# Attention with a routed expert layer: choice and placement of experts moved behind the next maxima on VectorE

## The chip, the cores and the metric

The kernel runs on one core of one Trainium2 chip. The metric is the device time of one execution in microseconds, lower is better. Five engines work side by side and meet only at semaphores: TensorE (PE in the rows, its weight loads PEld), VectorE (DVE), ScalarE (ACT), GpSimd (POOL) and SyncE (SP), which issues most transfers. Each engine does its own instructions strictly in the order in which they are written.

## The reference, cut to what matters

```python
x = x + xattn(layernorm(x), ctx, Wq, Wkv_expand, Wout)     # 32 batches of 112 rows, 512 wide, 16 heads, causal
x = x + ffn(layernorm(x), ...)

# in ffn, xf = all 3584 rows:
probs = softmax(xf @ gate_w.T, axis=1)                      # 8 experts
top_p, top_i = top_k(probs, 2)                              # two experts for each row
h = silu(xf @ fc1_e.T) * (xf @ fc2_e.T)                     # expert e, 352 wide
y = sum over the two experts of top_p * (h @ proj_e.T)
shared = (silu(xf @ s1.T) * (xf @ s2.T)) @ sp.T             # shared expert, 1408 wide
y = y + sigmoid(xf @ shared_gate.T) * shared
```

## The kernel before, in words

The program has three stages. The first does attention, the second layer norm, the router and the lists of rows for each expert. The second runs 63 tiles of 128 rows through their experts. The third does the shared expert and adds all up. Products are made from three fp32r products of high and low halves. The change touches the first stage alone, which lies between 0 and about 440 us.

The first stage is a software pipeline written out by hand. Its loop is `body(g)` on every engine: group g has four steps j = 0 to 3, and step (g, j) starts batch t = 4g + j; there are 8 groups with batches, and two more groups in which the rest drains while the shared expert's first block is computed. In one step TensorE does, in this order: the causal mask (line 925) and the scores (L935) of batch t, then for batch t - 1 the transposes of the exponentials (L944), of the inverse sums `rinv_wide` (L952) and the product with the values (L963), for batch t - 3 the transposes of the normed rows `xn` (L972), for batch t - 2 the output product (12 matmuls of L815), for batch t - 3 the router (L1001), then queries, keys and values of later batches (21 matmuls of L815). Once a group, at j = 2, `ranks` adds four small matmuls behind the router (L902, L903), which count the rows chosen before each row.

VectorE's `step(g, j)` does: the reciprocal of the last batch's sums (L1664); the maxima of the scores (`smax`, L1671, and `minus_max`, L1673), on which ScalarE's exponentials wait; `stats1` for the next batch (L1556, L1559); `rows_copy`, the copy of the normed rows out of PSUM (`xn2T`, L1629), on which the router waits; the low half of a later x; `attnT` (L1694); `x1` (L1703); `logits` and, at j = 2, the ranks' copy (L1642); `stats2`; the low half of `attnT` (L1715). At the end stands `choices(g, j)`: at j = 0 `choose(g - 1, 0)`, at j = 1 `choose(g - 1, 1)`, at j = 3 `place(g - 1)`. These are 10, 12 and 6 very small instructions on [112, 32] numbers, each of which waits for the one before. In group 7 they already stand behind the maxima of the following step.

GpSimd does in a step: `rinv_wide` (L1456), then `inverse_root` and `xn` of batch t - 3 (L1407, L1409, L1464), at j = 0 and 2 the halves of the context (L1418, L1420), `scaled_root` of batch t + 1 (L1407, L1409), and at j = 0 to 2, from group 3 on, three, three and two indirect transfers that write row numbers into the experts' lists (`scatter`, L1427); at j = 0 of groups 4 to 7 the row numbers are moved on first (L1436).

PSUM banks 4 to 7 are taken in turns. The table `TURNS` has for each result its bank and its place among the users of that bank, and `take` and `wait_emptied` count by it. The ranks' result lies in bank 4 before, behind the output product that `x1` reads. SyncE stores the routes of group g - 1 at the end of `body(g)`.

Of the kernel before, what the change touches and what calls it, by code (L numbers as in the profile page):

```python
# [62 lines left out]
class Turns:  # L63
# [5 lines left out]
    def there(self, g, j, lag):  # L69

        if j < 0 or lag is None:
            return g == 0
        return 0 <= g * TB + j - lag < self.batches
# [15 lines left out]
def build_program(nc, x, xT, ctxT, wq, wkv, wout, gates, w_experts, w_shared, out):  # L89
# [19 lines left out]
    with ctx:  # L109
# [382 lines left out]

        def is_last(n):

            return isinstance(n, int) and n == NG
# [56 lines left out]
        def _(sp):  # L552
# [41 lines left out]

            def body(g):
                for j in range(TB):
# [20 lines left out]
                    if there(g, j, 3):  # L617
# [12 lines left out]
                if routes(g):  # L630
                    sp.wait_ge(S["slots_ready"], g - 1)
                    sp.dma_start(route_rows[bass.ds(g - 2, 1)].rearrange("a s b f -> (a s) b f"),
                                 route_of(g - 1)[:, :, :]).then_inc(S["route_stored"], 16)
# [175 lines left out]
        def _(pe):  # L809
# [87 lines left out]
            def ranks(g, j):  # L897
# [3 lines left out]
                b = take(g, j, "rank")  # L901
# [193 lines left out]
            wait_emptied(pe, NG + 1, 2, "rank")  # L1095
# [275 lines left out]
        def _(pool):  # L1371
# [76 lines left out]
            def body(g):  # L1448
                for j in range(TB):
# [7 lines left out]
                    if there(g, j, 3):  # L1457
                        inverse_root(mv2, rs2, (j + 1) % 2, "stats2", "rstd2_made", t - 2)
                        if there(g, j, 5):
                            wait_filled(pool, g, j - 2, "normT")  # L1460
                            pool.wait_ge(xn2_stored[(j + 1) % 2], 16 * (2 * g + (j - 3) // 2))
                        pool.wait_ge(S["rstd2_made"], 2 * (t - 2))
                        settled(pool)
                        pool.tensor_scalar(xn2[:, (j + 1) % 2, :], x1[:, (j + 1) % 2, :], mv2[:, (j + 1) % 2, 0:1], rs2[:, (j + 1) % 2, 1:2],  # L1464
                                           ALU.subtract, ALU.mult).then_inc(S["xn2_ready"], 1)
# [6 lines left out]
                    if routes(g - 1) and before(g, NG + 1):  # L1472
                        if j == 0:
                            if isinstance(g, int) and g == 3:
                                pool.wait_ge(S["lists_zeroed"], 16)
                            else:
                                move_ids(g - 3)
                        if j < 3:
                            scatter(g - 2, ITEMS[3 * j:3 * j + 3])
                if isinstance(g, int) and g >= NG:  # L1480
# [70 lines left out]
        def _(dve):  # L1551
# [79 lines left out]
            def logits_out(g, j):  # L1631
# [5 lines left out]
                if j == 2 and routes(g):  # L1637

                    b = turns.bank("rank")
                    wait_filled(dve, g, j, "rank")  # L1640
# [16 lines left out]
            def step(g, j):  # L1657
# [16 lines left out]
                if is_late(g) and (g == NG - 1 or (g == NG and j == 0)):  # L1674
                    choices(*((g, j - 1) if j else (g - 1, TB - 1)))
# [41 lines left out]
                if is_late(g, 0) or not is_late(g, 2) or (j < TB - 1 and not is_late(g)):  # L1717
# [67 lines left out]
            def place(n):  # L1785

                link, count = chain("slot_step", (n - 1) * SLOT_STEPS)
                wait_emptied(dve, n + 1, 2, "rank")
# [308 lines left out]
```

## Time and profile before

| | us |
|---|---|
| median of 3 runs | 1524.58 (1521.63 to 1526.14) |
| the profiled execution | 1526.51 |
| its span, first to last instruction | 1524.7 |
| TensorE busy in the span | 1483.0 (97%) |
| VectorE, ScalarE, GpSimd busy | 854.7, 653.7, 585.3 |

The profiled execution is 0.1% above the median, inside the range of the runs. The granted TensorE clock over the span is 0.997 of full speed. Times in the rows are microseconds from the span's start, and engine names are those given above. "Step (4, 1)" below is the stretch from the first `smax` instruction of that step to the first of the next one.

### The profile page before, as it was taken

To read this page: it belongs to the slowest core of one execution; us is meant where nothing else is said; L and a number is where in the kernel's file an instruction comes from. 1 tells how busy PE (TensorE), PEld (TensorE's weight loads), DVE (VectorE), ACT (ScalarE), POOL (GpSimd) and SP (SyncE) were. 2 spreads that over 40 slices of the span, in tenths; PEclk is the share of its full clock that TensorE was granted. 3 is DMA by queue.
4 is the path that set the end of the run, shared out by engine and by line. 5 is a ranking of instruction groups with operands and counts; after the bars stand their busy time and mean duration, and the time that the engine had idled before them with its cause. 6 is when DMAs were issued, how large, how long until landed. Compare 5 with 4: busy or idle time off the path is not lost.

```text
span 1524.7 us, 28281 instructions
## 1 busy us (share of the span) xinstructions
PE 1483.0 (97%) x10026; PEld 1257.6 (82%) x10026; DVE 854.7 (56%) x1460; ACT 653.7 (43%) x1836; POOL 585.3 (38%) x503
## 2 busy tenths in 40 slices
PE   7999999999989999999999999999999999999999
PEld 5787777777778899999999999887888888888887
DVE  5566667667665578877867867545223322233322
ACT  6998888888864323333332332432111111111111
POOL 3333446545553277865865965112100001000010
PEclk9999999999999999999999999999999999999999
DMA  7244455545346489867778765553213012030110
GB/s 242 67 117 116 98 112 102 112 106 119 81 113 138 105 325 340 282 239 272 283 244 278 251 219 186 193 198 98 86 28 111 28 48 77 14 110 28 62 49 28
DMA packets 102905, 217.44 MB, mean 143 GB/s; under 512 B 43696, under 2 KB 48816, under 8 KB 98064
## 3 DMA queue, kind: packets, MB, share of 16 engines
q1 hardware_dynamic: 91184, 184.71, 38.8%
q0 software_dynamic: 11616, 31.35, 7.1%
q8 instruction: 63, 1.03, 0.3%
q14 instruction: 42, 0.34, 0.1%
HBM read 168.86 MB, written 47.17 MB: 142 GB/s over the span
## 4 chain that ended last, share of the span: by engine, by line
PE 81%; ACT 6%; issue 6%; DVE 4%; POOL 2%; DMA 1%; SPq 0%; DVEq 0%; POOLq 0%; ACTq 0%
PE psum L815 60%; PE psum L1134 11%; ACT probs L1239 4%; PE psum L894 2%; PE psum L1036 2%; PE psum L935 1%; PE psum L1060 1%; ACT probsT L1228 1%; PE psum L944 1%; POOL xn L1464 1%; DVE smax L1671 1%; PE psum L972 1%; PE psum L1001 1%; PE psum L963 0%; PE psum L925 0%
## 5 line engine op out<-in xcount | busy, mean ns | idle before, releaser
L1544 POOL DMA_INDIRECT routed<-expert_out_dram,slot_b x56 | 56.4, 1007 | 480.2 <-DVE slot_b L1993 327.9
L1239 ACT ACTIVATE probs<-psum,minus_max,rs 112x112 f32<-112x112 f32 x512 | 222.7, 511 | 2.4 <-DVE minus_max L1673 2.4
L2011 DVE TENSOR_TENSOR h_s<-psum,silu_s 128x512 f32<-128x512 f32 x66 | 45.7, 692 | 302.9 <-PE psum L815 298.6
L815 PE MATMUL psum<-nT_hi,ws_hi 128*128 128x512 f32 x528 | 209.4, 397 | 3.2 <-DVE nT_lo L1934 2.9
L815 PE MATMUL psum<-nT_lo,ws_hi 128*128 128x512 f32 x528 | 209.4, 397 | 0.0
L815 PE MATMUL psum<-nT_hi,ws_lo 128*128 128x512 f32 x528 | 209.2, 396 | 0.0
L1516 POOL DMA_INDIRECT xg<-normed_dram,tile_ids x63 | 149.9, 2380 | 35.7 <-DMA tile_ids<-lists_dram 12.7
L815 PE MATMUL psum<-wj_hi,gT_hi 128*128 128x352 f32 x504 | 162.8, 323 | 0.0
L815 PE MATMUL psum<-wj_hi,gT_lo 128*128 128x352 f32 x504 | 162.3, 322 | 0.0
L815 PE MATMUL psum<-wj_lo,gT_hi 128*128 128x352 f32 x504 | 161.8, 321 | 0.0
L1359 ACT ACTIVATE silu_s<-psum 128x512 f32<-128x512 f32 x66 | 39.4, 598 | 244.1 <-PE psum L815 244.1
L1239 ACT ACTIVATION_READ_ACCUMULATOR probs<-psum,minus_max,rs 112x1 f32 x512 | 139.7, 273 | 0.0
L1362 ACT ACTIVATE hs_hi<-h_s 128x512 fp32r<-128x512 f32 x66 | 41.7, 632 | 200.4 <-DVE h_s L2011 200.4
L1919 DVE TENSOR_TENSOR wj_lo<-wj_raw,wj_hi 128x2816 fp32r<-128x2816 f32 x35 | 121.6, 3476 | 8.9 <-POOL wj_hi L1499 7.2
L815 PEld LDWEIGHTS psum<-nT_hi,ws_hi 128*128 128x128 f32 x528 | 99.6, 189 | 27.6 <-DVE nT_lo L1934 3.4
L815 PEld LDWEIGHTS psum<-nT_hi,ws_lo 128*128 128x128 f32 x528 | 99.6, 189 | 24.0
L1499 POOL TENSOR_SCALAR wj_hi<-wj_raw 128x2816 fp32r<-128x2816 f32 x34 | 87.3, 2569 | 83.4 <-issue 76.1
L815 PEld LDWEIGHTS psum<-nT_lo,ws_hi 128*128 128x128 f32 x528 | 99.5, 188 | 23.5
L1134 PE MATMUL psum<-ws_lo,hs_hi 128*128 128x512 f32 x264 | 103.4, 392 | 0.0
L1134 PE MATMUL psum<-ws_hi,hs_hi 128*128 128x512 f32 x264 | 103.3, 391 | 0.0
L1134 PE MATMUL psum<-ws_hi,hs_lo 128*128 128x512 f32 x264 | 102.9, 390 | 0.0
L815 PEld LDWEIGHTS psum<-wj_lo,gT_hi 128*128 128x128 f32 x504 | 94.9, 188 | 2.6
(253 smaller groups left out, 3426.2 us busy)
## 6 DMA issues: line engine op xcount, KB each, us to landing
wj_raw<-in_w_experts SPq DMA_DIRECT2D x35, 1408.0 KB
wj_raw<-in_w_experts SPq DMA_DIRECT2D x35, 768.0 KB, 5.7
wj_raw<-in_w_shared SPq DMA_DIRECT2D x22, 768.0 KB, 5.5
expert_out_dram<-y_c SPq DMA_DIRECT2D x63, 256.0 KB
base<-x_dram SPq DMA_DIRECT2D x8, 1024.0 KB, 5.8
xT_raw<-in_xT SPq DMA_DIRECT2D x32, 224.0 KB, 5.5
x_in<-in_x SPq DMA_DIRECT2D x32, 224.0 KB, 5.4
x_res<-in_x SPq DMA_DIRECT2D x32, 224.0 KB
```

Source lines behind the costliest of these rows:

```text
L815: mm = pe.matmul(out_ap, u, v, start=(n == 0), stop=(n == last))
L894: mm = pe.matmul(bank(j), u, v, start=(c == 0 and q == 0), stop=(c == SC - 1 and q == 2))
L1036: mm = pe.transpose(psum[:, XT_BANK, c * P:(c + 1) * P], xg[b][:, c * P:(c + 1) * P], ident[:, :])
L1134: mm = pe.matmul(bank(j), u, v, start=(i == 0 and q == 0), stop=(i == SC - 1 and q == 2))
L1239: done = act.activation(probs[:, j % 2, 4 * r + m, :], psum[0:SEQ, r, m * SEQ:(m + 1) * SEQ], ACT.Exp, bias=minus_max[:, r, m:m + 1], scal ...
L1359: act.activation(silu_s[:, :], bank(b), ACT.Silu).then_inc(emptied_b[b], 1)
L1362: act.activation(hs_hi[:, i % 2, :], h_s[:, :], ACT.Copy).then_inc(S["hs_hi_made"], 1)
L1499: pool.tensor_scalar(wj_hi[b][:, FC_COLS], wj_raws[b][:, FC_COLS], 1.0, 0.0, ALU.mult, ALU.add).then_inc(S["wc_hi_made"], 1)
L1516: pool.indirect_dma_start(out=xg[b][:, :], out_offset=None, in_=normed_dram, in_offset=bass.IndirectOffsetOnAxis(ap=tile_ids[:, k % ROUND: ...
L1544: pool.indirect_dma_start(out=routed[:, b % 2, c, :], out_offset=None, in_=expert_out_dram, in_offset=bass.IndirectOffsetOnAxis(ap=slot_b[ ...
L1919: dve.tensor_tensor(wj_lo[b][:, FC_COLS], wj_raws[b][:, FC_COLS], wj_hi[b][:, FC_COLS].bitcast(F32), ALU.subtract).then_inc(S["wc_split"], 1)
L2011: dve.tensor_tensor(h_s[:, :], bank(b), silu_s[:, :], ALU.mult).then_inc(emptied_b[b], 1)
```

## The change

On VectorE, `choices` of a step now always stands behind the maxima of the following step, and no longer at the end of its own; group 7 and the first step of group 8 had this order already, so it is new for groups 2 to 6. On GpSimd, `inverse_root` and `xn` move from the second place of a step to its last: batch t - 2 at the end of step t, in place of batch t - 3 near the start of it. That puts them behind `scatter`. The ranks' result moves from bank 4 to bank 7, where it stands behind the product with the values, which `attnT` reads, and ahead of the keys. SyncE stores the routes of a group at j = 0 of a later group, behind the place where they are now made. TensorE's order stays as it was.

```diff
+              *([((_j, "rank", 0), "rank", 7)] if _j == 2 else []),
...
-        TURNS += [((_j, "rank", 0), 2 * TB, 4)]
+        TURNS += [((_j, "rank_tail", 0), "tail", 4)]
...
+            def store_routes(n):
+                sp.wait_ge(S["slots_ready"], n)
+                sp.dma_start(route_rows[n - 1], route_of(n)[:, :, :]).then_inc(S["route_stored"], 16)
...
+                    if j == 0 and 3 <= g <= NG:
+                        store_routes(g - 2)
...
-                if routes(g):
-                    sp.wait_ge(S["slots_ready"], g - 1)
...
+                if g >= NG:
+                    store_routes(g - 1)
...
-                    if there(g, j, 3):
-                        inverse_root(mv2, rs2, (j + 1) % 2, "stats2", "rstd2_made", t - 2)
-                        if there(g, j, 5):
-                            wait_filled(pool, g, j - 2, "normT")
...
+                    if there(g, j, 2):
+                        inverse_root(mv2, rs2, j % 2, "stats2", "rstd2_made", t - 1)
+                        if there(g, j, 4):
+                            wait_filled(pool, g, j - 1, "normT")
+                            pool.wait_ge(xn2_stored[j % 2], 16 * ((t - 2) // 2))
+                        pool.wait_ge(S["rstd2_made"], 2 * (t - 1))
...
-                if is_late(g) and (g == NG - 1 or (g == NG and j == 0)):
+                if t and (g < NG or (g == NG and j == 0)):
                     choices(*((g, j - 1) if j else (g - 1, TB - 1)))
...
-                if is_late(g, 0) or not is_late(g, 2) or (j < TB - 1 and not is_late(g)):
+                if is_late(g, 0):
                     choices(g, j)
```

VectorE before, at the end of step (2, 3) and the start of (3, 0); `rt_eq`, `route` and `slots_i` are the six instructions of `place`.

```order
L1715 TENSOR_TENSOR aT_lo<-attnT,aT_hi 128x448
L1792 TENSOR_TENSOR rt_eq<-rt_rank,rt_one 112x32
L1793 TENSOR_REDUCE route<-rt_eq 112x4
L1794 CAST slots_i<-route 112x4
L1792 TENSOR_TENSOR rt_eq<-rt_rank,rt_one 112x32
L1793 TENSOR_REDUCE route<-rt_eq 112x4
L1794 CAST slots_i<-route 112x4
L1664 RECIPROCAL rinv<-rsum 112x16
L1671 TENSOR_REDUCE smax<-psum 112x8
```

The same place of VectorE after (line numbers are 12 higher there).

```order
L1676 RECIPROCAL rinv<-rsum 112x16
L1683 TENSOR_REDUCE smax<-psum 112x8
L1685 TENSOR_SCALAR minus_max<-smax,rs 112x8
L1683 TENSOR_REDUCE smax<-psum 112x8
L1685 TENSOR_SCALAR minus_max<-smax,rs 112x8
L1804 TENSOR_TENSOR rt_eq<-rt_rank,rt_one 112x32
L1805 TENSOR_REDUCE route<-rt_eq 112x4
L1806 CAST slots_i<-route 112x4
L1804 TENSOR_TENSOR rt_eq<-rt_rank,rt_one 112x32
L1805 TENSOR_REDUCE route<-rt_eq 112x4
L1806 CAST slots_i<-route 112x4
L1568 BN_STATS stat<-x_in 112x6
```

The six instructions stood ahead of the reciprocal and the maxima and now stand between the maxima and `stats1`; the two halves of `choose` move in the same way.

GpSimd before, step (4, 0) from its `rinv_wide` to that of step (4, 1); the `DMA` row is `scatter`.

```order
L1456 COPY rinv_wide<-rinv 112x512
L1407 TENSOR_SCALAR rs<-mv 112x1
L1409 TENSOR_TENSOR rs<-rs,neg_half 112x1
L1464 TENSOR_SCALAR xn<-x,mv,rs 112x512
L1418 TENSOR_SCALAR ctx_hi<-ctx_in 128x224
L1420 TENSOR_TENSOR ctx_lo<-ctx_in,ctx_hi 128x224
L1407 TENSOR_SCALAR rs<-mv 112x1
L1409 TENSOR_TENSOR rs<-rs,neg_half 112x1
L1436 TENSOR_SCALAR token_id<-token_id 112x4
L1427 DMA lists_dram<-token_id,slots_i 28672x1 x3
L1456 COPY rinv_wide<-rinv 112x512
```

The same stretch of GpSimd after.

```order
L1468 COPY rinv_wide<-rinv 112x512
L1430 TENSOR_SCALAR ctx_hi<-ctx_in 128x224
L1432 TENSOR_TENSOR ctx_lo<-ctx_in,ctx_hi 128x224
L1419 TENSOR_SCALAR rs<-mv 112x1
L1421 TENSOR_TENSOR rs<-rs,neg_half 112x1
L1448 TENSOR_SCALAR token_id<-token_id 112x4
L1439 DMA lists_dram<-token_id,slots_i 28672x1 x3
L1419 TENSOR_SCALAR rs<-mv 112x1
L1421 TENSOR_TENSOR rs<-rs,neg_half 112x1
L1490 TENSOR_SCALAR xn<-x,mv,rs 112x512
L1468 COPY rinv_wide<-rinv 112x512
```

`xn` and the two small instructions that make its scale have moved from ahead of the context and the transfers to directly ahead of the next step's `rinv_wide`.

## Rows read from the trace of the kernel before

**Rows 1.** The page: the chain that ended last, by line.
```profile
PE psum L815 60%; PE psum L1134 11%; ACT probs L1239 4%; PE psum L894 2%; PE psum L1036 2%; PE psum L935 1%; PE psum L1060 1%; ACT probsT L1228 1%; PE psum L944 1%; POOL xn L1464 1%; DVE smax L1671 1%; PE psum L972 1%; PE psum L1001 1%; PE psum L963 0%; PE psum L925 0%
```
**Rows 2.** Stretches: start:end, length, busy per engine (instructions), PEclk, DMA share, GB/s.
```profile
99.32:111.72 12.40, 12.39 (x147) 10.26 (x146) 7.76 (x18) 11.39 (x42) 4.82 (x9) 1.00 0.47 133
230.18:243.69 13.51, 12.49 (x147) 10.26 (x146) 9.53 (x25) 11.61 (x42) 9.31 (x13) 1.00 0.36 73
243.69:256.89 13.20, 12.51 (x148) 10.34 (x147) 9.66 (x27) 11.61 (x42) 7.25 (x9) 1.00 0.66 133
256.89:271.34 14.45, 12.91 (x151) 10.67 (x150) 8.21 (x20) 11.61 (x42) 9.96 (x14) 1.00 0.69 111
271.34:283.73 12.39, 12.38 (x147) 10.28 (x146) 8.51 (x22) 11.60 (x44) 1.75 (x3) 1.00 0.48 121
364.01:378.48 14.47, 12.97 (x151) 10.71 (x150) 9.35 (x21) 11.77 (x42) 9.93 (x14) 1.00 0.55 116
124.12:391.01 266.89, 252.08 (x2922) 207.91 (x2921) 178.78 (x455) 232.95 (x851) 130.88 (x176) 1.00 0.48 109
```
**Rows 3.** Waits of TensorE over the whole span: us in total, times, longest.
```profile
PE psum L972 <- POOL xn L1464: 14.4, 15, 1.7
...
PE psum L902 <- DVE x L1703: 1.6, 6, 0.3
```
**Rows 4.** Order of time, step (1, 2): start, length, engine, line, what.
```profile
99.32 1.09 DVE L1671 TENSOR_REDUCE smax<-psum 112x8 f32<-112x896 f32 x1 [1.58 <-PE psum L935]
...
100.87 0.57 PE L952 MATMUL psum<-ident,rinv_wide 112*128 112x112 f32 x4
...
101.85 0.69 DVE L1556 BATCH_NORM_STATS2 stat<-x_in 112x6 f32<-112x512 f32 x1
...
105.50 0.86 PE L1001 MATMUL psum<-gates_sb,xn2T 128*112 128x9 f32 x8
```
**Rows 5.** Order of time, step (0, 3), TensorE.
```profile
65.07 0.60 PE L972 MATMUL psum<-ident,xn 112*128 112x112 f32 x4 [1.57 <-POOL xn L1464]
```
**Rows 6.** Order of time, step (7, 1), VectorE and TensorE.
```profile
406.60 0.18 DVE L1757 TENSOR_REDUCE rt_s<-rt_e 112x4 f32<-112x32 f32 x1
...
408.79 0.69 DVE L1556 BATCH_NORM_STATS2 stat<-x_in 112x6 f32<-112x512 f32 x1
...
409.77 0.62 DVE L1629 COPY xn2T<-psum 128x448 f32<-128x448 f32 x1
...
410.54 0.92 PE L1001 MATMUL psum<-gates_sb,xn2T 128*112 128x9 f32 x8 [0.37 <-DVE xn2T L1629]
```
**Rows 7.** Order of time, step (4, 2), TensorE at the ranks.
```profile
265.46 0.35 PE L902 MATMUL psum<-rt_pick,before_f 112*112 112x32 f32 x2 [0.28 <-DVE x L1703]
```
**Rows 8.** Order of time, step (6, 2), VectorE.
```profile
367.39 1.21 DVE L1852 TENSOR_TENSOR fc_lo<-wj_raw,fc_hi 128x1024 fp32r<-128x1024 f32 x1
...
369.50 0.62 DVE L1629 COPY xn2T<-psum 128x448 f32<-128x448 f32 x1
```
**Rows 9.** Order of time, steps (4, 0) and (4, 1), GpSimd.
```profile
235.46 0.19 POOL L1407 TENSOR_SCALAR rs<-mv 112x1 f32<-112x1 f32 x1
...
240.31 1.34 POOL L1427 DMA_INDIRECT lists_dram<-token_id,slots_i  x1 [0.30 <-issue]
243.40 0.61 POOL L1456 COPY rinv_wide<-rinv 112x512 f32<-112x512 f32 x1 [1.76 <-issue]
244.10 0.19 POOL L1407 TENSOR_SCALAR rs<-mv 112x1 f32<-112x1 f32 x1
...
245.26 2.08 POOL L1464 TENSOR_SCALAR xn<-x,mv,rs 112x512 f32<-112x512 f32 x1 [0.31 <-PE psum L944]
247.75 0.19 POOL L1407 TENSOR_SCALAR rs<-mv 112x1 f32<-112x1 f32 x1 [0.41 <-issue]
...
251.78 0.94 POOL L1427 DMA_INDIRECT lists_dram<-token_id,slots_i  x1 [0.30 <-issue]
```
**Rows 10.** Order of time, step (8, 1), GpSimd.
```profile
449.73 2.61 POOL L1464 TENSOR_SCALAR xn<-x,mv,rs 112x512 f32<-112x512 f32 x1 [0.31 <-POOL rs L1409]
```

More of the change, by code:

```diff
@@ L72, in there @@
             return g == 0
+        if lag == "rank":
+            return 2 <= g < self.batches // TB
+        if lag == "tail":
+            return g >= self.batches // TB
         return 0 <= g * TB + j - lag < self.batches
@@ L491, in groups, with rank_at @@
                 body(g)
+        def rank_at(g):
+            return "rank" if g < NG else "rank_tail"
         def is_last(n):
@@ L629, in body @@
                         load_x(t + TB)
-                if routes(g):
-                    sp.wait_ge(S["slots_ready"], g - 1)
-                    sp.dma_start(route_rows[bass.ds(g - 2, 1)].rearrange("a s b f -> (a s) b f"),
-                                 route_of(g - 1)[:, :, :]).then_inc(S["route_stored"], 16)
+                if g >= NG:
+                    store_routes(g - 1)
             groups(body)
@@ L900, in ranks @@
                 pe.wait_ge(S["choice_ready"], g - 1)
-                b = take(g, j, "rank")
+                b = take(g, j, rank_at(g))
                 pe.matmul(bank(b, SEQ, TB * EXPERTS), before_f[:, :], rt["pick"][:, :, :].rearrange("p b e -> p (b e)"), start=True, stop=False)
@@ L1094, in _ @@
             pe.wait_ge(S["table_ready"], 1)
-            wait_emptied(pe, NG + 1, 2, "rank")
+            wait_emptied(pe, NG + 1, 2, "rank_tail")
             pe.wait_ge(h1_emptied, SC)
@@ L1456, in body @@
                         pool.tensor_copy(rinv_wide[:, :, :], rinv[:, :].unsqueeze(2).to_broadcast([SEQ, HEADS, HD])).then_inc(S["rinv_spread"], 1)
-                    if there(g, j, 3):
-                        inverse_root(mv2, rs2, (j + 1) % 2, "stats2", "rstd2_made", t - 2)
-                        if there(g, j, 5):
-                            wait_filled(pool, g, j - 2, "normT")
[L1461 to L1465, printed above, removed]
                     if j == 0 and before(g, NG):
@@ L1479, in body @@
                             scatter(g - 2, ITEMS[3 * j:3 * j + 3])
+                    if there(g, j, 2):
[4 more added lines that the diff above has]
+                        pool.wait_ge(S["rstd2_made"], 2 * (t - 1))
+                        settled(pool)
+                        pool.tensor_scalar(xn2[:, j % 2, :], x1[:, j % 2, :], mv2[:, j % 2, 0:1], rs2[:, j % 2, 1:2],
+                                           ALU.subtract, ALU.mult).then_inc(S["xn2_ready"], 1)
                 if isinstance(g, int) and g >= NG:
@@ L1637, in logits_out @@
                 if j == 2 and routes(g):
-                    b = turns.bank("rank")
-                    wait_filled(dve, g, j, "rank")
+                    b = turns.bank(rank_at(g))
+                    wait_filled(dve, g, j, rank_at(g))
                     at_least(dve, S["slot_step"], (g - 2) * SLOT_STEPS)
@@ L1787, in place @@
                 link, count = chain("slot_step", (n - 1) * SLOT_STEPS)
-                wait_emptied(dve, n + 1, 2, "rank")
+                wait_emptied(dve, n + 1, 2, rank_at(n + 1))
                 if not (isinstance(n, int) and n == 1) and not is_last(n):
```

## The prediction

> **What bounds the kernel now.** I read the page's chain first. TensorE's lines lead it, and only three entries of the first stage are not TensorE's own work: the exponentials, `xn` and `smax` [rows 1]. The change touches the first stage alone, so I cut that stage into steps, from one `smax` to the next. A step without any of the moved work takes 12.40 us, of which TensorE is busy 12.39, at a granted clock of 1.00 (the first of [rows 2]). That is the floor: an order of instructions on other engines cannot go below it. ScalarE is busy 11.4 to 11.6 of it and has little room, but it isn't last.
>
> The four steps of group 4 take 13.51, 13.20, 14.45 and 12.39 us [rows 2]. Together that is 53.55, or 3.95 above four floors. The row for all twenty steps of groups 2 to 6 says 266.89 us, 18.9 above twenty floors of 12.40. This is what there is to win, and about 0.4 us in each group is the ranks' own matmuls (12.91 busy in place of some 12.5), which stay: 2.0 in all.
>
> Next I looked for what TensorE waits for. Over the whole span it waits 14.4 us in 15 places for `xn` of GpSimd, and 1.6 us ahead of the ranks for `x1` [rows 3]. In the steps concerned VectorE does `choose` before the reciprocal; `rinv_wide` waits for the reciprocal, and `xn` is queued behind `rinv_wide`. So one late VectorE instruction delays both the maxima and the transposes of `xn`. `place`, at the end of j = 3, costs nothing now: that step is at 12.39.
>
> **The change part by part.** I write T for the start of `smax` in a step.
>
> *Maxima and reciprocal.* With `choose` behind the maxima, neither is late any more, and `xn` is made a step ahead. The waits for `xn` go, and so does the lateness of `smax`. If nothing else came up, every step would be at its floor of 12.40, with 0.4 more where the ranks are. The question is what the moved pieces now delay, and there are three things.
>
> *Router.* VectorE's `xn2T` copy now stands behind `choose`. In a step without stalls `stats1` starts at T + 2.53 and the router's matmuls at T + 6.18 [rows 4]. Group 7 shows the new order already: the first half of `choose` takes 408.79 - 406.60 = 2.19 us, from `stats1` to the copy are 0.98, the copy is 0.62, and TensorE starts 0.15 behind its end, after a wait of 0.37 for it [rows 6]. So the router could start at T + 2.53 + 2.19 + 0.98 + 0.62 + 0.15 = T + 6.47, which is 0.3 late. In that step of group 7 the maxima took 0.3 longer than in rows 4, which gives 0.6; I take 0.45. The second half has two instructions more, so about 0.3 more: 0.75. `place` has 6 instead of 10 instructions, 1.3 us: T + 5.6, no wait. Bounds for each router wait are 0.2 and 1.0.
>
> *Ranks.* They need bank 7, that is `attnT`, which at j = 2 comes behind the second half of `choose`, the copy (starting at T + 6.2) and the low half of x, each of the two some 0.6 long. `attnT` ends near T + 8.0, the ranks start 0.15 later, and the router would let them go at T + 6.18 + 0.75 + 0.71 = T + 7.65. The wait is 0.5, in place of 0.28 [rows 7]. In bank 4 it would have been `x1`, 0.7 later still. The keys, which now need the ranks' copy, come 2.5 us behind the ranks, and the copy follows them within 0.6: no wait. Step j = 2 becomes 12.40 + 0.75 + 0.5 + 0.4 = 14.05.
>
> *GpSimd.* `xn` now waits behind `scatter`, and the next `rinv_wide` behind `xn`. In step (4, 0) the scale of the next batch starts at T + 5.28 (235.46 - 230.18), and the last transfer ends at T + 11.07 to T + 11.47 [rows 9]. After the change the start is the same, since VectorE's `stats1` then ends near T + 5 (2.53 for the maxima, 1.3 for `place`, 1.0). Behind that come 1.16 (244.10 to 245.26), 2.08 for `xn`, and 0.61 for `rinv_wide`, with 0.1 of gap: T + 15.0. TensorE wants `rinv_wide` at 1.55 into the next step (100.87 - 99.32), T + 13.95 [rows 4]. It waits 1.1 us, in steps (4, 1), (5, 1) and (6, 1). The router wait of the same step lies inside it, since the transposes come earlier. Bounds are 0 (were the indirect transfers and `xn` to overlap) and 2.0. In step (3, 0) no row numbers are moved, which saves 1.2, and the wait is gone. At j = 1 the three transfers end at T + 9.0 now; with `choose` ahead of `stats1` they end at T + 10.9, `rinv_wide` at T + 14.8, and TensorE wants it at T + 13.5 + 1.55 = T + 15.05. That fits narrowly. At j = 2 and 3 there is room.
>
> *Group 6.* VectorE has extra pieces for the shared expert behind the maxima there. In step (6, 2) the copy starts at T + 5.49 already (369.50 - 364.01), with `fc_lo` of 1.21 in front [rows 8]. With 2.5 more for `choose` the router starts at T + 8.75, 2.6 late; ranks included the step is 15.4, where it is 14.47 now. This step gets slower by 0.9.
>
> *Start and end.* In step (0, 3) TensorE waits 1.57 for `xn` [rows 5]; `xn` is now made in the step before, and I count 1.4. Group 7 keeps VectorE's order, but GpSimd's changes: `rinv_wide` of (7, 1) comes nearly 2 us later. TensorE has no queries there and has slack, so I count 0.4, between 0 and 2. Routes stored later cost nothing: the next use of that buffer is a step away, 12.40 us.
>
> **The sum**, step lengths in order of j, before against after:
> - group 2: 52.5 (18.9 less four times 4.0 leaves 3 above the floors) against 12.40 + 12.85 + 14.05 + 12.40 = 51.7: -0.8.
> - group 3: 53.55 against 51.7: -1.85.
> - groups 4 and 5: 53.55 against 12.40 + 13.5 + 14.05 + 12.40 = 52.35: -1.2 each, -2.4.
> - group 6: 53.7 against 12.40 + 13.5 + 15.4 + 12.5 = 53.8: +0.1.
> - step (0, 3) -1.4, group 7 +0.4.
>
> That is -5.95 us. The later stages are bound by TensorE and only shift. The profiled execution, 1526.5 us, would be 1520.5; it lies 1.9 above the median, which goes from 1524.6 to **1518.6**.
>
> A rule of the Trainium skill (SBUF — State Buffer, section Who interferes with whom) speaks against the new order: a VectorE instruction with two SBUF inputs contends with a GpSimd instruction that reads SBUF. The trace agrees at one place: `xn` took 2.61 us in step (8, 1) where 2.08 is usual [rows 9, 10]. By this rule `xn`, which now runs beside the low half of `attnT` and no longer beside maxima out of PSUM, would be up to 0.5 us longer in each step. It matters only in the steps in which TensorE waits for `rinv_wide`.
>
> **The rivals.**
> A. The whole excess goes: router and `rinv_wide` wait for nothing. 18.9 - 2.0 + 1.4 = 18.3 us less, 1506.3. For it: TensorE is 97% busy and the old waits are plain. Against it: group 7 shows the router waiting behind `choose` [rows 6], and nothing overlaps GpSimd's transfers with its computing.
> B. The gain is eaten: the moved pieces cost what they saved. Router and ranks waits at their upper bounds (0.3 more in each of ten steps, 3 us) and 1 us more at `rinv_wide` in three steps give -5.95 + 6 = 0, 1524.6. For it: group 6 comes out even in my own sum.
> C. Slower: GpSimd becomes the bound of j = 0, 1 and 2. Its queue is `rinv_wide`, context, scale, transfers, `xn`, one behind the other. At j = 1 it is within 0.3 us of TensorE. If a transfer takes 1.34 us, as the longest in rows 9, and not 0.94, and `xn` 2.6 [rows 10], a step with three transfers has 1.7 us more. TensorE then waits 1.7 more in eight steps (groups 3 to 6, j = 0 and 1), nearly 13.6 us at most; the router waits hide about 2, which gives -5.95 + 11.6 = +5.7, 1530.3. It decides from about 0.75 us more per step on.
> D. The order does not do what it says, because the exponentials, not the maxima, are the limit. ScalarE is busy 11.6 of 12.4, so the floor stands at 12.40 either way, and this gives B's time.
>
> **How the numbers follow.** Forecast 55%, A 12%, B with D 23%, C 10%. About 0.3% (4.6 us) is what a measurement of this kernel can tell from no change. Below 1520.0 lie A and, with its own spread of 1514 to 1522, most of the forecast's share: 0.12 + 0.46, and a little of B: 0.60. Above 1529.2 lie C's larger part: 0.08. The rest is 0.32. The range reaches from 1510, short of A, to 1525.5, past B, and leaves out most of A and C.
>
> **What would show it.** Steps (g, 0) at 12.40 for g = 2 to 6, with no waits of L972 for `xn` in the whole trace. Waits of the router for `xn2T` of about 0.5 at j = 1 of groups 2 and 3 and 0.75 at j = 2. TensorE waiting about 1 us at its `rinv_wide` transposes in steps (4, 1), (5, 1), (6, 1), with `xn` on GpSimd directly ahead. Step (6, 2) longer than before, near 15.4. The forecast is wrong if (g, 1) stays at 12.40, which is A, or if `rinv_wide` waits stand at j = 0, 2 or 3 too, which is C.

## The result, and the profile after

| | before | after |
|---|---|---|
| median | 1525.36 us (4 runs, 1521.63 to 1526.72) | 1550.6 us (4 runs, 1548.55 to 1553.31) |
| profiled execution | 1526.51 | 1550.07 |
| its span | 1524.7 | 1548.3 |
| granted TensorE clock over the span | 0.997 | 0.983 |
| TensorE busy | 1483.0 | 1497.8 |

The ratio is 1.017, with an interval of 1.0146 to 1.0195. The changed kernel is 25 us slower. I had forecast 6 us faster, with a range of 1510.0 to 1525.5.

The waits of TensorE in the changed kernel (columns: who waits, for whom, us in total, times, longest):

```profile
PE psum L1013 <- DVE xn2T L1641: 14.2, 8, 3.9
PE psum L964 <- POOL rinv_wide L1468: 13.6, 9, 3.9
...
PE psum L984 <- DVE logits L1648: 3.1, 1, 3.1
...
PE psum L914 <- DVE attnT L1706: 0.6, 4, 0.2
```

Against [rows 3] the waits for `xn` of GpSimd have gone, as forecast, and those ahead of the ranks (L914) are small. In their place the router (L1013) waits 14.2 us for `xn2T`, and the transposes of the inverse sums (L964) 13.6 us for `rinv_wide`. The forecast had both, but smaller: 0.45 or 0.75 us at a time for the router (2.6 in one step), and 1.1 us in three steps for `rinv_wide`. The list for VectorE names what it had not:

```profile
DVE smax L1683 <- PE psum L947: 58.7, 29, 5.6
...
DVE rt_s L1769 <- DMA route_dram<-route: 19.9, 6, 4.9
```

`rt_s` is the first instruction of `choose`. It waits six times, 19.9 us in all, for a transfer: the store of the routes of the group before. No instruction of VectorE waited for that store before. Step (3, 1) shows where, on VectorE in order of time (start, length, engine, line, what, and in brackets the idle time ahead and who ended it):

```profile
188.21 0.23 DVE L1685 TENSOR_SCALAR minus_max<-smax,rs 112x8 f32<-112x8 f32 x1
191.95 0.19 DVE L1769 TENSOR_REDUCE rt_s<-rt_e 112x4 f32<-112x32 f32 x1 [3.51 <-DMA route_dram<-route]
...
194.15 0.69 DVE L1568 BATCH_NORM_STATS2 stat<-x_in 112x6 f32<-112x512 f32 x1
195.00 0.18 DVE L1571 BATCH_NORM_AGGREGATE mv<-stat 112x2 f32<-112x6 f32 x1 [0.16 <-DVE stat L1568]
195.13 0.62 DVE L1641 COPY xn2T<-psum 128x448 f32<-128x448 f32 x1
```

The maxima are done at 188.4. VectorE then stands 3.51 us, and all that is queued behind stands with it: the rest of `choose`, `stats1`, and the `xn2T` copy. TensorE in the same step:

```profile
187.85 0.60 PE L964 MATMUL psum<-ident,rinv_wide 112*128 112x112 f32 x4 [0.49 <-POOL rinv_wide L1468]
...
195.90 1.63 PE L1013 MATMUL psum<-gates_sb,xn2T 128*112 128x9 f32 x8 [3.22 <-DVE xn2T L1641]
```

The router waits 3.22 us. Its eight matmuls then take 1.63 us, where they took 0.86 in [rows 4]. SyncE shows why the store is late:

```profile
180.91 0.33 SPq L624 DMA_DIRECT2D x_dram<-x  x1
181.28 0.43 SPq L627 DMA_DIRECT2D x_res<-in_x  x1
181.76 0.44 SPq L631 DMA_DIRECT2D normed_dram<-xn  x1
182.24 0.54 SPq L634 DMA_DIRECT2D normedT_dram<-xn2T  x1
182.83 0.65 SPq L605 DMA_DIRECT2D route_dram<-route  x1
```

Step (3, 0) starts at 173.4. The store is queued in it behind the store of `x1`, which SyncE can issue only when the output product has been added up, at 180.91. So the routes' store is issued 9.4 us into a step of 12.4. And it takes long to land. Of the five such stores that are issued in groups 3 to 7 the view of that line says (us from issue to landing, shortest, median, longest):

```profile
DMA to landing us min/median/max: 6.9/8.0/9.0
```

Over all seven stores of that buffer the list of transfers says 7.5, where the kernel before had 2.9 for the same 12.2 KB (transfers, size of one, us to landing). First before, then after:

```profile
route_dram<-route SPq DMA_DIRECT2D x7, 12.2 KB, 2.9
```

```profile
route_dram<-route SPq DMA_DIRECT2D x7, 12.2 KB, 7.5
```

9.4 and 8 make 17.4 us, while the next `choose` reaches its place at 12.4 + 2.6 = 15.0. This first store takes longest, 9.1 us (191.95 less 182.83), which makes the 3.51 us of the wait.

The stretches that answer to [rows 2] (start:end, length, busy per engine, then granted clock, DMA share, GB/s) are steps (3, 0) to (3, 3):

```profile
173.42:185.82 12.40, 12.39 (x147) 10.27 (x146) 8.47 (x21) 11.44 (x42) 6.75 (x11) 1.00 0.40 78
185.82:205.03 19.21, 15.50 (x147) 12.70 (x146) 9.17 (x25) 11.77 (x42) 10.09 (x13) 0.82 0.70 121
205.03:218.79 13.76, 13.17 (x151) 10.65 (x150) 9.89 (x31) 11.67 (x42) 6.64 (x9) 1.00 0.27 64
218.79:231.15 12.36, 12.35 (x147) 10.22 (x146) 7.76 (x15) 11.67 (x44) 4.01 (x6) 1.00 0.52 133
```

Three of the four steps are within 0.3 us of the forecast (12.40, 14.05 and 12.40). One is not: (3, 1) takes 19.21 us, 6.0 more than before. TensorE is idle for 3.7 of it, 3.0 more than before. The other 3.0 are in its busy time, 15.50 in place of 12.5, for as many matmuls. Cut at the change of clock the same step reads:

```profile
185.82:195.20 9.38, 6.37 (x68) 4.81 (x66) 5.30 (x17) 8.95 (x37) 1.98 (x2) 1.00 0.73 107
195.20:202.00 6.80, 6.10 (x20) 5.62 (x21) 3.87 (x9) 0.78 (x3) 5.25 (x8) 0.50 0.48 137
202.00:205.03 3.03, 3.03 (x60) 2.27 (x59) 0.00 (x0) 2.04 (x4) 2.87 (x4) 0.98 1.06 127
```

From 195.2 to 202.0, from the late part of the router's wait on, the granted clock is 0.50: 1.2 GHz in place of 2.4. So a wait of 3.22 us costs 6.3 us: without it the step takes 12.88 (a1 below).

Step lengths in us, from one `smax` to the next, of the kernels that follow (a1 to c2 are named in the next section):

| step | before | forecast | after | a1 | a4 | b1 | b5 | b3 | c2 |
|---|---|---|---|---|---|---|---|---|---|
| (0,3) | 13.59 | 12.2 | 11.77 | 11.77 | 11.77 | 13.60 | 13.59 | 11.76 | 11.77 |
| (3,0) | 13.49 | 12.40 | 12.39 | 12.35 | 12.53 | 21.69 | 12.43 | 12.35 | 12.35 |
| (3,1) | 13.20 | 12.85 | 19.21 | 12.88 | 12.95 | 16.21 | 12.70 | 12.36 | 13.65 |
| (3,2) | 14.48 | 14.05 | 13.76 | 13.82 | 12.76 | 13.78 | 14.06 | 13.84 | 12.15 |
| (4,1) | 13.20 | 13.5 | 19.79 | 13.12 | 12.84 | 16.29 | 13.04 | 12.38 | 13.63 |
| (5,1) | 13.20 | 13.5 | 14.21 | 13.23 | 12.85 | 15.45 | 13.06 | 12.36 | 13.64 |
| (6,1) | 13.20 | 13.5 | 17.53 | 13.33 | 13.08 | 15.04 | 13.67 | 13.18 | 13.55 |
| (6,2) | 14.47 | 15.4 | 16.68 | 16.84 | 12.98 | 13.46 | 17.05 | 16.52 | 12.63 |
| (7,1) | 12.11 | 12.5 | 14.14 | 14.14 | 12.61 | 13.26 | 11.58 | 11.28 | 11.28 |
| groups 2 to 5, sum | 213.2 | 208.1 | 220.6 | 208.1 | 206.0 | 245.1 | 210.4 | 207.6 | 203.6 |
| group 6, sum | 53.70 | 53.8 | 59.28 | 55.09 | 52.58 | 62.02 | 55.73 | 54.61 | 51.09 |

### The profile page after: what moved, and what is told of

The parts are those of the page before. It is cut to its first block, busy times and chain, and to the rows that moved or that the text cites. A ratio compares the mean times of both kernels' runs of the same rounds, so it can differ in the third digit from the quotient of the medians.

```text
span 1548.3 us, 28286 instructions
## 1 busy us (share of the span) xinstructions
PE 1497.8 (97%) x10026; PEld 1269.0 (82%) x10026; DVE 854.1 (55%) x1460; ACT 656.1 (42%) x1836; POOL 583.7 (38%) x503
## 4 chain that ended last, share of the span: by engine, by line
PE 68%; issue 1%; DVE 1%; DMA 1%; POOL 0%; SPq 0%; ACT 0%; DVEq 0%; POOLq 0%; ACTq 0%
PE psum L827 52%; PE psum L1146 11%; PE psum L906 2%; PE psum L1048 2%; PE psum L1072 1%; DMA route_dram<-route 0%; DMA routed<-expert_out_dram,slot_b 0%; DVE base L2011 0%; DVE base L2050 0%; DVE nT_lo L1946 0%; PE psum L975 0%; POOL routed L1556 0%; PE psum L1013 0%; PE psum L984 0%; DVE fc_lo L1864 0%
## 5 line engine op out<-in xcount | busy, mean ns | idle before, releaser
L1528 POOL DMA_INDIRECT xg<-normed_dram,tile_ids x63 | 150.2, 2384 | 35.5 <-DMA tile_ids<-lists_dram 12.7
L1683 DVE TENSOR_REDUCE smax<-psum 112x8 f32<-112x896 f32 x64 | 69.5, 1086 | 58.7 <-PE psum L947 58.7
```

Of the source, the lines that this page charges most:

```text
L1528: pool.indirect_dma_start(out=xg[b][:, :], out_offset=None, in_=normed_dram, in_offset=bass.IndirectOffsetOnAxis(ap=tile_ids[:, k % ROUND: ...
L1683: dve.tensor_reduce(smax[:, 2 * i:2 * i + 2, :], scores, AX.X, ALU.max).then_inc(S["smax_made"], 1)
```

## The experiments

Each kernel ran on a chip beside the kernel before; ratios are to it.

**a1, two route buffers.** The changed kernel, with a second buffer for the routes of odd groups, so that `choose` waits for the store before the last one and not for the last.

```diff
-            return route_last if is_last(n) else route
+            return route_last if is_last(n) else route_odd if n % 2 else route
...
-                if not (isinstance(n, int) and n == 1) and not is_last(n):
-                    dve.wait_ge(S["route_stored"], 16 * (n - 1))
+                if n >= 3 and not is_last(n):
+                    dve.wait_ge(S["route_stored"], 16 * (n - 2))
```

> The changed kernel with two route buffers taken in turns, so that the first half of choose waits for the store of two groups back and not of the last one. Theory R (the late route store: VectorE stood 3.5, 4.4, 1.4, 2.5 and 3.2 us before the first instruction of choose in groups 3 to 7, and TensorE's clock fell behind the stalls): that wait goes, steps (3,1) to (6,1) come to 12.7 to 13.5 us, the half-speed stretches in the first stage are mostly gone, and the time is the one first forecast, 1515 to 1520. Theory G (GpSimd is the bound, since xn stands behind the list transfers and rinv_wide behind xn): nothing changes there, 1545 to 1551.

Measured: 1523.96 us (12 runs; before 1523.99), ratio 0.9997, interval 0.9986 to 1.0008. That is above the 1515 to 1520 expected. VectorE no longer waits for the store. TensorE's waits are:

```profile
PE psum L965 <- POOL rinv_wide L1469: 11.9, 11, 2.8
...
PE psum L1014 <- DVE xn2T L1642: 3.4, 4, 1.7
```

The step of the example, and (6, 2) and (7, 1):

```profile
185.48:198.36 12.88, 12.39 (x148) 10.26 (x147) 9.24 (x26) 11.62 (x42) 7.53 (x10) 1.00 0.83 164
...
355.39:372.23 16.84, 14.61 (x152) 11.93 (x151) 11.15 (x33) 11.78 (x42) 9.27 (x12) 0.90 0.48 106
...
396.01:410.15 14.14, 11.45 (x136) 9.22 (x134) 8.90 (x25) 10.72 (x40) 8.45 (x13) 0.88 0.24 29
```

The whole loss of the changed kernel, 27 us, hangs on that one wait: the store still lands as late (6.7 and 8.0 us at the median for the two buffers), but nobody waits for it.

**a2, the store ahead.** The changed kernel with the routes' store issued first in step (g, 0), ahead of the store of `x1`.

```diff
+                    if j == 0 and 3 <= g <= NG:
+                        store_routes(g - 2)
                     if there(g, j, 2):
                         wait_emptied(sp, g, j, "proj")
...
-                    if j == 0 and 3 <= g <= NG:
-                        store_routes(g - 2)
```

> The changed kernel with the route store issued on SyncE ahead of the x1 store of step (g,0), not behind the normedT store. The store then leaves some 4.5 us earlier (as soon as place is done, near T + 4). Theory R: it lands 3 to 9 us later, at T + 7 to T + 13, and choose wants it at T + 15, so little or nothing is waited for: 1515 to 1525. If a store of these small rows takes long for another reason than its place in the queue, choose still waits, by 0 to 2 us a group. Theory G: 1545 to 1551.

Measured: 1526.01 us (12 runs), ratio 1.0009, interval 0.9997 to 1.002, 1 us above the range expected. VectorE doesn't wait for the store here either. The first store is issued at 178.0 in place of 182.8, and it lands sooner too:

```profile
route_dram<-route SPq DMA_DIRECT2D x7, 12.2 KB, 2.5
```

2.5 us in place of 7.5, with the same bytes. So the long landing was made by the place in the queue, behind four transfers of 224 KB, and not by the transfer's own shape. The new place is also 4.8 us earlier in time; no run tells the order in the queue from what else moves at that moment. Either cure alone, a buffer or a place, takes away the 25 us.

**a3, GpSimd as before.** The changed kernel with GpSimd's old order.

```diff
+                    if there(g, j, 3):
+                        inverse_root(mv2, rs2, (j + 1) % 2, "stats2", "rstd2_made", t - 2)
...
-                    if there(g, j, 2):
-                        inverse_root(mv2, rs2, j % 2, "stats2", "rstd2_made", t - 1)
```

> The changed kernel with GpSimd's order of before (xn second in a step, ahead of the list transfers); VectorE, SyncE and the banks as in the changed kernel. Theory R: the wait of VectorE for the route store stays, so the time stays slow, 1545 to 1560. Theory G: the loss comes from GpSimd's order, and the time falls to that of before or below, 1515 to 1527.

Measured: 1549.13 us (4 runs), ratio 1.0163, interval 1.0128 to 1.0197. The loss is there without GpSimd's new order, and `rt_s` waits for the store as long:

```profile
DVE rt_s L1769 <- DMA route_dram<-route: 21.4, 6, 7.0
```

So rival C, GpSimd as the bound, is not the cause, though a slower kernel was its forecast.

**b1, the late store alone.** The kernel before, with nothing changed but the place of the routes' store.

```diff
+                    if j == 0 and 3 <= g <= NG:
+                        store_routes(g - 2)
...
-                if routes(g):
-                    sp.wait_ge(S["slots_ready"], g - 1)
...
+                if g >= NG:
+                    store_routes(g - 1)
```

> The kernel before with only SyncE's part of the change: routes of group g - 2 are stored at j = 0 of group g behind the normedT store, while choose stands at the end of its step and xn near the start, as before. Theory R: the store leaves near T + 9 of step (g,0) and lands 3 to 9 us later, while VectorE comes to choose at T + 10.6 of the same step, so it stands 2 to 7 us in each of groups 3 to 6 and the reciprocal and the maxima with it; stretches at half clock follow. 1540 to 1560. Theory G (the place of the store costs nothing): 1521 to 1527.

Measured: 1572.36 us (4 runs), ratio 1.0323, interval 1.0298 to 1.0349: slower still, and more than I had expected. `choose` stands at the end of step (g, 0) here, where VectorE reaches it half a microsecond behind the issue of the store (189.9 and 189.4 in step (3, 0)):

```profile
DVE rt_s L1761 <- DMA route_dram<-route: 44.7, 6, 9.3
```

Steps (3, 0) and (3, 1) of this kernel (the cuts are within 0.1 us of the `smax` instructions):

```profile
179.30:200.96 21.66, 13.96 (x161) 11.53 (x159) 9.46 (x26) 13.47 (x46) 8.48 (x11) 0.91 0.55 88
200.96:217.17 16.21, 14.66 (x131) 11.62 (x132) 9.71 (x29) 9.88 (x38) 7.67 (x10) 0.70 0.25 53
```

One moved transfer of 12.2 KB costs 49 us in a kernel that is otherwise untouched. That is the mechanism by itself. VectorE's new order, with `choose` a step later, had hidden about half of it.

**a4, GpSimd's order alone.** The kernel before, with `inverse_root` and `xn` at the end of GpSimd's step, and nothing else.

```diff
-                    if there(g, j, 3):
-                        inverse_root(mv2, rs2, (j + 1) % 2, "stats2", "rstd2_made", t - 2)
...
+                    if there(g, j, 2):
+                        inverse_root(mv2, rs2, j % 2, "stats2", "rstd2_made", t - 1)
...
```

> The kernel before with only GpSimd's new order: xn and its scale last in a step. Theory R: TensorE's 14.4 us of waits for xn mostly go, a wait of about 1 us for rinv_wide comes at j = 1 of groups 4 to 6, and smax stays late behind choose: 1514 to 1524, nowhere slow. Theory G: slower than before by 15 to 25 us, 1540 to 1551.

Measured: 1516.76 us (6 runs), ratio 0.9953, interval 0.9934 to 0.9972. This part of the change is faster than before by itself. TensorE's waits:

```profile
PE psum L952 <- POOL rinv_wide L1456: 10.4, 12, 2.8
...
PE psum L902 <- DVE x L1703: 2.5, 6, 0.7
```

Steps (g, 0) of groups 3 to 6 fall from 13.5 to 12.5 here, with `choose` as late as before. In (3, 0) TensorE idles for 0.01 us. So what made these steps long was `xn`, and the lateness of the maxima by itself doesn't hold TensorE there.

**b5, VectorE's part without GpSimd's.** a1 with GpSimd's old order: `choose` behind the maxima, bank 7 and two buffers.

```diff
+                    if there(g, j, 3):
+                        inverse_root(mv2, rs2, (j + 1) % 2, "stats2", "rstd2_made", t - 2)
...
-                    if there(g, j, 2):
-                        inverse_root(mv2, rs2, j % 2, "stats2", "rstd2_made", t - 1)
...
```

> The changed kernel with two route buffers and GpSimd's order of before: choose behind the maxima and the ranks in bank 7, nothing else. Theory V (choose behind the maxima wins by itself, since smax and rinv_wide are never late): the waits for xn at j = 1 and 2 go although xn stands in its old place; router waits of 0.4 to 0.8 remain, and the list transfers no longer hold rinv_wide back: 1515 to 1521. Theory W (VectorE's new order brings what it costs, the router waiting for the xn2T copy and half-speed stretches behind such waits): 1521 to 1528.

Measured: 1524.27 us (12 runs), ratio 1.0012, interval 1.0 to 1.0023. VectorE's new order brings nothing to the time: it ends the waits for `xn` only in part and puts the router's in their place.

```profile
PE psum L1014 <- DVE xn2T L1642: 7.5, 9, 2.5
...
PE psum L985 <- POOL xn L1477: 4.6, 4, 1.6
```

By steps, each part ends the same lateness. Group 3, which has no half-speed stretch in any of the three, takes 53.56 us before, 51.23 with GpSimd's part (a4), 51.55 with VectorE's (b5) and 51.42 with both (a1): the second adds nothing to the first. What b5 loses against a4, 7.5 us over groups 2 to 6, lies mostly in groups 2, 5 and 6 (1.0, 2.5 and 3.1 us). In step (g, 2) of each of the three its router waits for `xn2T`, and the granted clock stands at 0.50 for about 3 us behind that.

**b2, choices behind the copy.** a1 with `choose` and `place` not ahead of `stats1` and the `xn2T` copy but behind them.

```diff
-                if t and (g < NG or (g == NG and j == 0)):
-                    choices(*((g, j - 1) if j else (g - 1, TB - 1)))
...
                     rows_copy(g, j)
+                if t and (g < NG or (g == NG and j == 0)):
+                    choices(*((g, j - 1) if j else (g - 1, TB - 1)))
```

> The changed kernel with two route buffers, and choose and place behind the xn2T copy in a step, not directly behind the maxima; VectorE has about 1.3 us of idle time there, before attnT. Theory W: the router's waits of 0.4 to 1.7 us at j = 1 and 2 go, fewer half-speed stretches follow, and it beats the version with two route buffers alone by 4 to 9 us: 1515 to 1520. Theory G (rinv_wide behind xn is what eats the gain): the waits for rinv_wide stay and with them nearly all of the time, 1521 to 1525.

Measured: 1519.97 us (12 runs), ratio 0.9978, interval 0.9964 to 0.9992. The router's wait is gone from the list. `attnT` is late in its place, and the ranks with it, 6.3 us in all. The time is inside what was expected for the first theory, at its upper end.

**b3, transfers spread.** b2 with two indirect transfers in each of the four steps in place of three, three, two and none.

```diff
-                        if j < 3:
-                            scatter(g - 2, ITEMS[3 * j:3 * j + 3])
+                        scatter(g - 2, ITEMS[2 * j:2 * j + 2])
```

> As the last, and the eight list transfers of a group go two to a step over all four steps, not three, three and two. Theory W: xn ends 1.25 us sooner at j = 0 and 1, rinv_wide is waited for no more in groups 4 to 6, and some 1 us of each of these groups is won on top: 1511 to 1517, the best of all. Theory G: it is here that the gain comes, 6 us or more below the version without the spread.

Measured: 1519.17 us (12 runs), ratio 0.9976, interval 0.9965 to 0.9987. The 1511 to 1517 expected are missed.

```profile
PE psum L965 <- POOL rinv_wide L1469: 6.4, 5, 2.8
PE psum L915 <- DVE attnT L1706: 6.3, 6, 2.0
```

The waits for `rinv_wide` fall from 9.0 in b2 to 6.4, steps (3, 1), (4, 1) and (5, 1) stand at 12.36 to 12.38, and (7, 1) at 11.28. The time does not tell the two kernels apart: their intervals overlap.

**c1, GpSimd's order and bank 7.** a4 with the ranks in bank 7.

```diff
+              *([((_j, "rank", 0), "rank", 7)] if _j == 2 else []),
...
-        TURNS += [((_j, "rank", 0), 2 * TB, 4)]
+        TURNS += [((_j, "rank_tail", 0), "tail", 4)]
```

> GpSimd's new order and the ranks in bank 7; VectorE's order and the place of the route store are those of before. In a4_pool_alone (GpSimd's order alone) TensorE waited 2.5 us in all ahead of the ranks for x1. If what is left of the ranks' wait is the bank, those 2.5 us go and nothing else changes: about 1514.5 us, ratio 0.994, with the half-speed stretches as few as there (none or one in the first stage). If the bank is worth nothing because the waits for rinv_wide take its place, 1516.8 as in a4_pool_alone.

Measured: 1515.87 us (5 runs; before 1522.14), ratio 0.9965, interval 0.9951 to 0.9978. The wait ahead of the ranks has gone, and steps (2, 2), (3, 2) and (5, 2) fall from 12.73 to 12.76 in a4 to 12.16 to 12.22. Groups 2 to 6 take 254.8 us where a4 has 258.6. But (7, 1) is 15.35 here and 12.61 in a4, and the ratios overlap: the expected 2 us are in the steps and can't be told in the time.

**c2, second half early.** b3 with the second half of `choose` at the end of step (g, 1), as before the change, so that nothing of it stands ahead of `attnT` in (g, 2).

```diff
-                if t and (g < NG or (g == NG and j == 0)):
+                if t and (g < NG or (g == NG and j == 0)) and (is_late(g) or j != 2):
                     choices(*((g, j - 1) if j else (g - 1, TB - 1)))
...
-                if is_late(g, 0):
+                if is_late(g, 0) or (j == 1 and not is_late(g)):
                     choices(g, j)
```

> As b3_behind_copy_spread (two route buffers, choices behind the copy of the normed rows, two transfers in each of four steps), but the second half of choose stands at the end of step j = 1, as in before, so that nothing of it lies ahead of attnT and the ranks at j = 2. If the excess of step (g, 2), 13.85 us in b3 against 12.73 in a4_pool_alone, is the ranks waiting for attnT behind the second half, the step falls to 12.7 to 12.9 with (g, 0), (g, 1) and (g, 3) at 12.4, the first stage is 5 us shorter than in b3 and 4 us shorter than in a4, and TensorE keeps its clock: 1512 to 1514 us. If the second half at the end of j = 1 delays the next maxima, (g, 2) stays near 13.5 and the time is that of b3, 1519.

Measured: 1513.08 us (5 runs), ratio 0.9939, interval 0.9926 to 0.9953. This is the lowest time of all and inside what was expected, though its interval overlaps those of a4, c1 and c3, and the steps are not those expected. (3, 0) to (3, 3):

```profile
174.38:186.73 12.35, 12.34 (x147) 10.27 (x147) 8.42 (x21) 11.39 (x42) 6.89 (x10) 1.00 0.40 71
186.73:200.38 13.65, 13.64 (x160) 11.55 (x160) 11.64 (x37) 12.21 (x44) 6.45 (x9) 1.00 0.75 140
200.38:212.53 12.15, 11.51 (x139) 9.38 (x137) 8.23 (x20) 10.90 (x41) 7.94 (x11) 1.00 0.50 129
212.53:224.88 12.35, 12.34 (x147) 10.26 (x147) 7.82 (x15) 11.60 (x44) 6.32 (x9) 1.00 0.44 78
```

(3, 1) has 160 matmuls in place of 147, and TensorE idles 0.01 us in it: the next `smax` is late by 1.3, behind the second half of `choose`, while TensorE already works on. The cut from `smax` to `smax` moves, and the two steps have to be read together: 25.80 us, where b3 has 26.20 and before 27.68. From the first `smax` to that of (7, 3) c2 takes 386.2 us, b3 392.4, a4 390.2 and before 401.3.

**c3, c2 without the spread.**

```diff
-                        scatter(g - 2, ITEMS[2 * j:2 * j + 2])
+                        if j < 3:
+                            scatter(g - 2, ITEMS[3 * j:3 * j + 3])
```

> As c2_second_half_early, with the transfers three, three and two in steps 0 to 2 as in before. If GpSimd's length at j = 0 and 1 is what TensorE's waits for rinv_wide come from, (g, 1) is 12.9 to 13.2 and not 12.4, and the time 2 to 3 us above c2. If the waits of b2_behind_copy (9.0 us for rinv_wide) cost nothing beside the others, it equals c2.

Measured: 1514.82 us (5 runs), ratio 0.9946, interval 0.9932 to 0.996. Groups 2 to 6 take 255.0 us, in c2 254.7, and (7, 1) 13.42 in place of 11.28. The difference to c2, 1.7 us, is inside the intervals. Steps (g, 1) of groups 3 to 6 take 13.5 to 13.8 us, not the 12.9 to 13.2 expected: the cut at a late `smax` moves here as in c2.

**The clock, over all runs.** Each run comes with its mean granted clock. Over 61 runs of the kernel before, the time falls with it: on average 1528.4 us at 0.993 (4 runs), 1524.8 at 0.996 (14), 1521.1 at 0.999 (13). A line through them has 1.16 us for each 0.001, with a correlation of -0.96. Mean clocks, and the time that each kernel would have at the 0.9967 of before, taking those 1.16 us for all of them (an estimate; c1 and c2 ran on another chip, where before had a median of 1522.1):

| | before | after | a1 | a4 | b1 | b5 | b3 | c1 | c2 |
|---|---|---|---|---|---|---|---|---|---|
| mean clock | 0.9967 | 0.9848 | 0.9918 | 0.9952 | 0.9788 | 0.9924 | 0.9938 | 0.9938 | 0.9958 |
| median, us | 1523.7 | 1550.6 | 1524.0 | 1516.8 | 1572.4 | 1524.3 | 1519.2 | 1515.9 | 1513.1 |
| at 0.9967, us | 1523.7 | 1536.8 | 1518.3 | 1515.0 | 1551.6 | 1519.3 | 1515.8 | 1512.5 | 1512.0 |

The last row is rough. Lines through the twelve runs of a kernel have 1.10 to 1.14 us for each 0.001 in a1, b5 and b2, but 0.5 to 0.6 in a2 and b3, and for after and b1 the line reaches far beyond the clocks that it was drawn from (0.993 to 0.999). By it 13.8 of the 27 us between after and before would go with the clock and 13.1 would be the waits. The two profiled executions say the same in kind: TensorE is busy 14.8 us longer (1497.8 for 1483.0) and idle 8.8 us longer.

## Why the prediction was wrong

**The step that failed** is the last sentence on group 7: "Routes stored later cost nothing: the next use of that buffer is a step away, 12.40 us." I took the distance from the step in which the store stands to the step of the next `choose`, and set nothing against it. What I left out:
- where in its step SyncE gets to the store: 9.4 us in, behind a transfer that waits for the output product;
- how long it takes to land: 2.9 us in the trace of before, 8.0 in its new place;
- that the waiting instruction had moved too, to 2.6 us into its step.

The first and the last could be read before. In step (3, 0) of the kernel before SyncE reaches that place 10.2 us in (186.80 less 176.62), 2.9 more is 13.1, and the next `choose` would come at 13.5 + 2.6 = 16.1: the store would have been in time by 3 us. So the reading would not have turned the forecast by itself. But it would have shown a margin of 3 us, on a landing time taken from another place in the queue, where I had written 12.40. That margin was a rival worth a chance, and I gave it none. a1, a2 and b1 settle the cause: without the wait the loss is gone (a1), with the store ahead of the queue it is gone (a2), and with the moved store alone it is there and larger (b1).

**What held.** In a1 the rest of the sum can be read without the wait:
- Groups 2 to 5: forecast 213.2 - 5.05 = 208.15, measured 208.14. That the two agree so closely is luck: (5, 2) is 1.4 us over its forecast, with a half-speed stretch, and the other steps together are as much under theirs. Step (g, 0) is at 12.35 to 12.5 in all groups, (g, 1) at 12.7 to 13.3, (g, 2) at 13.7 to 14.1 in groups 2 to 4.
- TensorE waits for `rinv_wide` in (4, 1), (5, 1) and (6, 1), 0.72, 0.85 and 0.81 us for the forecast's 1.1. It also waits 0.49, 0.50 and 0.52 us for it in (3, 1), (3, 2) and (6, 2), where the forecast had room. There is no wait for `xn` of GpSimd.
- The router waits 0.74 us in (2, 2), for 0.75, and 0.42 in (4, 2); in (3, 2) of the changed kernel it waits 0.42. The ranks wait 0.16 or 0.17 us, for 0.5. The router's wait of 0.45 us at j = 1 of groups 2 and 3 isn't there: (3, 1) is near its forecast, 12.88 for 12.85, by the wait for `rinv_wide` that the forecast didn't have.

**Terms that were mis-sized.**
- Step (0, 3): -1.8 for -1.4.
- (6, 2): 16.84 in a1 for 15.4. The router's wait is smaller than forecast, 1.71 for 2.6, but the clock is at 0.90 over the step [a1's rows above], and TensorE's busy time 14.6 in place of 13.0.
- (7, 1): +2.0 us in a1, where I had counted 0.4 and at most 2. TensorE waits 2.69 us for `rinv_wide`, which GpSimd makes behind three transfers and `xn`; step (7, 0) takes 11.2 us in place of 12.7, so it is wanted sooner. But the wait isn't what was mis-sized. a4 waits as long at the same place, its clock doesn't fall, and its step takes 12.61, +0.5, near the forecast's +0.4. The other 1.5 us are the clock. First a1, then a4:

```profile
400.15 0.98 PE L965 MATMUL psum<-ident,rinv_wide 112*128 112x112 f32 x4 [2.69 <-POOL rinv_wide L1469]
```

```profile
395.27 0.60 PE L952 MATMUL psum<-ident,rinv_wide 112*128 112x112 f32 x4 [2.71 <-POOL rinv_wide L1456]
```

Spreading the transfers takes the wait away (b3, c2: 11.28). Over (7, 0), (7, 1) and (7, 2) together a1 is 0.15 us shorter than before, since the first and the last gain 1.5 and 0.7.

**The clock**, which my sum did not have at all. In the trace of a1 it falls in (0, 1), (5, 2), (6, 2) and (7, 1), and costs some 1.5 us in each of the last three (an estimate, from (7, 1) in a1 and a4). But these steps are already in the sums above: from the first `smax` to that of (7, 3) a1 takes 396.6 us for 401.3, 4.6 less, and its span is 5.4 us shorter (1519.3 for 1524.7), near the 5.95 of the forecast. The median shows nothing of it, 1524.0 for 1524.0. The profiled execution of a1 is the second fastest of its twelve and has the highest clock of them, 0.994, where the others are at 0.990 to 0.993. By the line above a1 would be at 1518.3 at the clock of before, 5.4 below it (an estimate). So the time that the steps gained is missing in executions with a lower clock, of which no trace was kept; where their clock falls stays open. A wait that replaces another of equal length isn't free if the clock falls behind it.

**The rivals.** A (1506.3) and C are out: in a1 router and `rinv_wide` do wait, a3 has the loss without GpSimd's new order, and that order alone is faster than before (a4). D is out as a reason for no gain, since steps (g, 0) went from 13.5 to 12.4. But they fall to 12.5 in a4 too, where `choose` still stands ahead of the maxima, so D is right that the maxima weren't the limit; whether the exponentials are wasn't tested. B gave 1524.6, the time of a1, but for another reason than it names: the waits of groups 2 to 5 that it wanted larger came to what I had summed, and the median lies higher where the clock is lower. None of the four had a transfer as the wait that replaces the old ones.

**The Trainium skill's rule in the forecast.** The rule of the Trainium skill (SBUF — State Buffer, Who interferes with whom) is that a VectorE instruction with two SBUF inputs contends with a GpSimd instruction that reads SBUF. The trace of the changed kernel agrees, but in most steps it is VectorE that pays. Twelve of the 32 `xn` start shortly before the low half of `attnT` and run beside all of it. They take 2.08 to 2.10 us as ever, and the low half takes 0.91 to 1.08 us in place of 0.63. Once, at 144.3, the low half starts first: it keeps its 0.63, and `xn` takes 2.27. The low half before, then after (ns, shortest, median, longest):

```profile
L1715 DVE TENSOR_TENSOR aT_lo<-attnT,aT_hi x32: 591/624/628, 46.5 to 447.1; 128x448 fp32r<-128x448 f32 x32
```

```profile
L1727 DVE TENSOR_TENSOR aT_lo<-attnT,aT_hi x32: 590/626/1081, 45.7 to 465.2; 128x448 fp32r<-128x448 f32 x32
```

So I had the contention right and its side wrong. It was worth nothing in the sum: `xn` isn't made later by it, and TensorE nowhere waits for the low half.

## What to carry to other kernels

A transfer that is moved has two dates: when its queue gets to it, and when it lands. Both are to be read at the new place, from what stands ahead of it there, and set against the moment at which the buffer is wanted again. Where the time from issue to that moment is near the longest landing in the trace, give the buffer a twin: 112 bytes a partition were worth 27 us here. And take a large rearrangement apart before it is kept or dropped: GpSimd's part alone was 0.5% faster than before, VectorE's brought nothing, and the store cost 3%.

## What the runs showed of the hardware

- A store of 12.2 KB lands 2.5 us after its issue ahead of four transfers and 7.5 to 8.0 behind them. Its issue on SyncE takes 0.65 us there in place of 0.34. The Trainium skill (DMA: Bandwidth & Descriptors, Queues, rings and completion order) says that each of the DMA engines takes the descriptors of one ring in order. The runs agree as far as they go: 2.5 us ahead of the four and 7.5 us behind them, though the earlier place is also an earlier moment.
- A wait of TensorE can cost more than its length. In the changed kernel 3.22 us of waiting in (3, 1) made the step 6.3 us longer than in a1, with the clock at 0.50 for 6.80 us. The clock can fall behind short waits too. Step (5, 2) of a1 took 15.43 us with no wait of more than 0.55:

```profile
301.88:317.31 15.43, 14.71 (x152) 12.06 (x150) 10.02 (x32) 11.62 (x42) 9.02 (x12) 0.89 0.66 139
```

- What decides whether the clock falls isn't settled. The same wait of 2.7 us in (7, 1) is followed by about 3.4 us at half speed in a1, by 6.8 in c1 and by none in a4. a4 waits for `rinv_wide` 12 times, 10.4 us, and its profile has no half-speed stretch in the whole first stage; c1 waits as often and as long, and has two of 6.8 us (at 390.6 and 424.8). No run here was made to tell that apart.
